# Cross-attention on one core: the token branch's last steps placed inside its loop and among the main branch's first tiles

## What is computed

```python
enc, ca = ctx[:, :2044], ctx[:, 2044:]            # ctx (2, 2048, 384), x (2, 1024, 640)
hs = mha(x @ Wq, enc @ Wk, enc @ Wv)              # 8 heads of 80
ca_q1 = einsum('btc,th->bch', ca, Wq_ca)[:, indices]   # 384 rows spread to 1024
ca_hs1 = mha(ca_q1, x, x)
ca_hs2 = mha(ca_hs1 @ Wq, ca @ Wk_ca, ca @ Wv_ca) # 4 keys
out = (hs + ca_hs2) @ Wout + b_out + x
```

## Time and profile before

| quantity | value |
|---|---|
| median of three runs | 1199.17 us |
| profiled execution, its own time | 1199.81 us |
| its span, first to last instruction | 1197.8 us |
| PE busy | 1189.5 us (99%) |
| DVE busy | 826.5 us (69%) |
| ACT busy | 680.4 us (57%) |
| POOL busy | 210.7 us (18%) |
| chain that ended last, PE's share | 95% |
| granted TensorE clock | 1.000 |

### The profile page before, as it was taken

The page is one execution under the profiler, slowest core; times in us unless marked ns, Lnnn a source line. Parts: engine busy times, 40 slices in busy tenths (PEclk is TensorE's granted clock), DMA queues, the critical chain, the costliest instruction groups (busy, mean ns, idle before and its releaser), DMA issues.

```text
span 1197.8 us, 14824 instructions
## 1 busy us (share of the span) xinstructions
PE 1189.5 (99%) x5649; PEld 965.1 (81%) x5649; DVE 826.5 (69%) x1181; ACT 680.4 (57%) x797; POOL 210.7 (18%) x123
## 2 busy tenths in 40 slices
PE   9999999999999999999999999999999999999999
PEld 7888888788666677888888888888888888888998
DVE  7468625771144388888888888888888888886551
ACT  5323433222644467777677777777777777778210
POOL 1100000011000021222222222222221221221233
PEclk9999999999999999999999999999999999999999
DMA  8975785693920084354454455445436436422254
GB/s 310 352 271 177 266 299 212 224 322 113 293 50 1 1 199 99 97 125 111 111 120 112 106 116 127 101 105 137 106 90 152 100 80 155 134 68 67 91 196 154
DMA packets 139376, 178.08 MB, mean 149 GB/s; under 512 B 79705, under 2 KB 97113, under 8 KB 135466
## 3 DMA queue, kind: packets, MB, share of 16 engines
q1 hardware_dynamic: 131690, 156.36, 46.1%
q0 software_dynamic: 2864, 10.24, 2.6%
q10 hardware_dynamic: 4752, 10.55, 2.6%
HBM read 113.72 MB, written 63.24 MB: 148 GB/s over the span
## 4 chain that ended last, share of the span: by engine, by line
PE 95%; DVE 2%; DMA 1%; issue 1%; ACT 1%; SPq 0%; DVEq 0%; ACTq 0%
PE at_ps L1330 28%; PE bank L726 20%; PE at_ps L1311 19%; PE at_ps L243 9%; PE acc_t_ps L1091 7%; PE at_ps L1520 6%; PE s_ps L1059 2%; PE bank L703 1%; DVE prob_lo L1186 1%; DMA x_f<-in_xT 1%; PE acc_t_ps L1070 1%; PE f_ps L243 1%; PE f_ps L1012 1%; PE f_ps L1022 0%; PE at_ps L1523 0%
## 5 line engine op out<-in xcount | busy, mean ns | idle before, releaser
L259 DVE TENSOR_REDUCE mpart<-at_ps 128x1 f32<-128x512 f32 x480 | 324.6, 685 | 90.8 <-PE at_ps L243 89.2
L1249 ACT ACTIVATE prob_hi<-at_ps 128x1024 fp32r<-128x1024 f32 (+1 forms) x256 | 263.3, 1028 | 178.9 <-PE at_ps L1311 176.8
L1330 PE MATMUL at_ps<-prob_hi,v 128*128 128x512 f32 (+1 forms) x1024 | 315.0, 393 | 0.0
L1186 DVE TENSOR_TENSOR prob_lo<-probs,prob_hi 128x1024 fp32r<-128x1024 f32 (+1 forms) x211 | 273.5, 1296 | 21.3 <-ACT probs L1254 20.7
L1254 ACT ACTIVATE probs<-at_ps 128x1024 f32<-128x1024 f32 (+1 forms) x256 | 261.6, 1022 | 0.0
L1330 PEld LDWEIGHTS at_ps<-prob_hi,v 128*128 128x128 f32 (+1 forms) x1024 | 191.1, 188 | 43.7 <-ACT x_hi_place L1263 1.7
L1186 POOL TENSOR_TENSOR prob_lo<-probs,prob_hi 128x1024 fp32r<-128x1024 f32 x45 | 108.0, 2400 | 501.6 <-ACT probs L1254 501.6
L243 PE MATMUL at_ps<-a 128*128 128x512 f32 x480 | 189.0, 394 | 0.4 <-DVE mpart L259 0.4
L1330 PE MATMUL at_ps<-prob_lo,v 128*128 128x512 f32 (+1 forms) x512 | 158.7, 391 | 0.5 <-DVE prob_lo L1186 0.5
L1311 PE MATMUL at_ps<-a 128*128 128x512 f32 (+1 forms) x512 | 158.7, 391 | 0.2 <-DVE vw L965 0.2
L1311 PE MATMUL at_ps<-b 128*128 128x512 f32 (+1 forms) x512 | 158.1, 390 | 0.0
(11 more groups left out here) (160 smaller groups left out, 1392.8 us busy)
## 6 DMA issues: line engine op xcount, KB each, us to landing
v_hi_d<-v_t SPq DMA_DIRECT2D x16, 648.0 KB, 6.3
v_lo_d<-v_t SPq DMA_DIRECT2D x16, 648.0 KB, 8.1
v<-v_hi_d SPq DMA_DIRECT2D x16, 648.0 KB, 5.5
v<-v_lo_d SPq DMA_DIRECT2D x16, 648.0 KB, 7.2
k_hi_d<-out_hi SPq DMA_DIRECT2D x40, 256.0 KB, 4.9
k_lo_d<-out_lo SPq DMA_DIRECT2D x40, 256.0 KB, 5.9
a<-k_hi_d SPq DMA_DIRECT2D x16, 640.0 KB, 7.6
b<-k_hi_d SPq DMA_DIRECT2D x16, 640.0 KB, 11.2
```

The costliest lines, as they stand in the source:

```text
L259: dve.tensor_reduce(self.mpart[:, g % 2, qt, c:c + 1], at[:, 0:w], AX, ALU.max).then_inc(self.mx_done, 1)
L1186: eng.tensor_tensor(pl[n % PL][0:r, :], prob[n % PF][0:r, :], ph[n % PB][0:r, :].bitcast(F32), ALU.subtract).then_inc(sem, 1)
L1249: act.activation(ph[n % PB][0:r, :], s_ps[n % 2][0:r, :], ACT.Exp, scale=SCALE).then_inc(ph_done, 1)
L1330: mm = pe.matmul(wide[3][:, u], a[0:r, t, :], y[0:r, u * CH:(u + 1) * CH], start=t == 0 and m == 0, stop=t == KT - 1 and m == 2)
```

## The change

- Maxima chunks start at token step 8 (`MAX_FROM` 2), and 16 chunks of head 1 (`AHEAD`) follow those of head 0, so that 49 steps carry one; the first two main steps carry none, the next ten one or two. Loads of the first two heads' `a` are issued earlier on SP. Chunks have 512 columns and last tiles 128 keys throughout; the four excess keys have zero values (`fill_ones` clears them, `load_v` leaves them out, with four DMAs a head for two).
- The gather of batch 1 stands in token step 57, in the maxima's PSUM banks (now one tensor, `f_both`); `fold_values` in steps 59 and 60. ACT's copies of them stand in the same steps.
- What is left of the token part (last token scores, last exponential, `weigh`, gather, copy) stands among main steps 0 and 1, as the functions of `TokensEnd`.
- `normalise` is two operations of 512 columns, at t = 10 and t = 11, each behind a wait for the low part of tile n + 1.
- `early_split` of t = 13 to 15 stands behind the last low part.

```diff
-MAX_FROM = 6
+MAX_FROM = 2
+GATHER_AT, VALUES_AT = 57, (59, 60)
+AHEAD = 16
-FIRST_PIECES = (2, 3, 2, 3, 3, 2, 3, 3, 2, 3, 3, 3)
+FIRST_PIECES = (0, 0, 1, 2, 1, 2, 1, 2, 1, 2, 2, 2)
...
-    def normalise(self, pool, g):
+    def normalise(self, pool, g, u):
         p = g % 2
+        half = slice(u * CH, (u + 1) * CH)
         pool.wait_ge(self.rbc_in, (g + 1) * 16)
-        pool.tensor_tensor(self.o_raw[p][0:D, :], self.o_raw[p][0:D, :], self.rbc[:], ALU.mult
+        pool.tensor_tensor(self.o_raw[p][0:D, half], self.o_raw[p][0:D, half], self.rbc[:, half], ALU.mult
                            ).then_inc(self.norm_done, 1)
...
@@ tokens, scalar
+                    if k == GATHER_AT:
+                        first_copy()
+                    if k in VALUES_AT:
+                        vw_out(VALUES_AT.index(k))
                 if n == NH:
-                    exp2(0)
+                    exp2(act, 0)
             raw_out(len(heads) - 1)
-            vw_out(0)
-            first_copy()
-            exp2(1)
-            vw_out(1)
...
@@ tokens, tensor, end of step k
+                if k == GATHER_AT:
+                    first_gather()
+                if k in VALUES_AT:
+                    fold_values(VALUES_AT.index(k))
-            pe.wait_ge(oh_done, 1)
-            pe.wait_ge(at.mx_done, STEPS)
-            fold_values(0)
-            token_scores(len(heads) - 1)
-            first_gather()
-            fold_values(1)
...
@@ attend, gpsimd
-                if t == 11 and g:
-                    at.normalise(pool, g - 1)
+                if t in (10, 11) and g:
+                    wait_low(pool, n + 1)
+                    at.normalise(pool, g - 1, t - 10)
...
@@ attend, scalar
             exp(0)
-            last_copy(act)
+            tokens_end.last_exp(act)
             exp(1)
+            tokens_end.last_copy(act)
...
@@ attend, vector
             split(0)
+            tokens_end.last_weigh(dve)
...
-                if g == G - 1:
+                if g == G - 1 and t < KT - 3:
                     early_split(dve, t)
+            for t in range(KT - 3, KT):
+                early_split(dve, t)
...
@@ attend, tensor
+            tokens_end.folded_values(pe)
+            scores(0, nothing)
+            tokens_end.last_scores(pe)
+            scores(1, nothing)
+            tokens_end.last_fold(pe)
+            values_high(0, nothing)
+            scores(2, nothing)
+            values_low(0)
+            values_high(1, nothing)
+            tokens_end.last_gather(pe)
+            scores(3, nothing)
+            values_low(1)
+            tokens_end.gathered(pe, B)
+            for n in range(2, N):
```

More of the change, by code:

```diff
@@ L779, in tokens @@
         raw = kept["raw"]
[L780 to L784, removed]
+        rden, s2, t2, r2 = kept["fold"]
+        f_both = s.psum("f_ps", [P, 2, CH])
+        f_ps = [f_both[:, i] for i in range(2)]
         s_ps = [s.psum(f"s_ps{i}", [P, 2, CH]) for i in range(2)]
@@ L997, in vector, with token_scores @@
                     if n == NH + 1:
-                        weigh(0, order[0])
-            low_vw(0)
+                        weigh(dve, 0)
+                if k in VALUES_AT:
+                    low_vw(VALUES_AT.index(k))
             fold(len(heads) - 1)
             center(order[1])
-            weigh(1, order[1])
-            low_vw(1)
+        def token_scores(pe, n):
+            b, h = heads[n]
+            if n == 0:
+                pe.wait_ge(wk2_done, B)
+            pe.wait_ge(raw_done, n + 1)
+            for c in range(KC):
+                mm = pe.matmul(t_ps[n % 2][:, c, :], raw[n % 2][:, c * P:(c + 1) * P],
+                               kept["wk2"][:, b, h, :], start=True, stop=True)
+            mm.then_inc(t_full, 1)
         def tensor(pe):
@@ L1114, in last_gather @@
             pe.wait_ge(p2_done, B)
-            pe.wait_ge(e_done, len(heads) * pairs)
             for c, a, z in spans:
@@ L1327, in values @@
                     for u in range(2):
-                        if t == 0 and m == 0 and g:
+                        if t == 0 and low == 0 and g:
                             pe.wait_ge(at.o_act, 2 * (g - 1) + u + 1)
-                        mm = pe.matmul(wide[3][:, u], a[0:r, t, :], y[0:r, u * CH:(u + 1) * CH],
-                                       start=t == 0 and m == 0, stop=t == KT - 1 and m == 2)
-                    if m < 2:
-                        between()
-                mm.then_inc(pv_done, 1)
@@ L1336, in tensor, with values_low @@
-            pe.wait_ge(at.kb_ones, 3)
-            gathered(pe, 1)
-            scores(0, lambda: None)
-            last_gather(pe)
-            folded_values(pe)
-            scores(1, lambda: None)
-            for n in range(N):
+                        pe.matmul(wide[3][:, u], v_s[g % 2][:, low, t, :], ph[n % PB][:, u * CH:(u + 1) * CH],
+                                  start=t == 0 and low == 0, stop=False)
+                    between()
+            def values_low(n):
+                g, t = divmod(n, KT)
+                wait_low(pe, n)
+                for u in range(2):
+                    mm = pe.matmul(wide[3][:, u], v_s[g % 2][:, 0, t, :], pl[n % PL][:, u * CH:(u + 1) * CH],
+                                   start=False, stop=t == KT - 1)
+                mm.then_inc(pv_done, 1)
@@ L1455, in gpsimd @@
                 add_bias(n)
-            at.normalise(pool, G - 1)
+            for u in range(2):
+                at.normalise(pool, G - 1, u)
             for n in range(2, NT_OUT):
@@ L1571, in program @@
         kept["p1_0"] = blocks(wq_flat[:, n_x:n_x + n_p], 2)
+        n_f = n_x + n_p
+        small = []
+        for shape in ((2, KC), (B, KC, HT), (B, KC * NH), (B, KC * NH)):
+            n = math.prod(shape)
+            flat = wq_flat[:, n_f:n_f + n]
+            names = "abc"[:len(shape)]
+            small.append(flat.rearrange(f"p ({' '.join(names)}) -> p {' '.join(names)}", **dict(zip(names, shape))))
+            n_f += n + -n % 8
+        assert n_f <= 2 * MC * HID
+        kept["fold"] = small
         kept["wkca"] = blocks(x_flat[:, 0:n_k], KC)
```

190 lines of the change are left out of this document (103 added, 87 removed).

## The result

The changed kernel takes **1225.95 us** (median of 4 runs, 1224.67 to 1227.83), the one before 1199.26 beside it: a ratio of 1.0224, 95% interval 1.0208 to 1.0240. The sign was forecast, the size was not: 1205.6 us, with a range that ended at 1207.5. The profiled execution took 1225.38 us. All times are medians of the runs that lie within 1.5% of their kernel's fastest, which leaves out one run, 1242.34 us of `e3_split_alone`.

A forecast was written before the change was run, and what follows sets the result against it. PE was taken to bound the kernel, so only removed matmuls or PE stops pay. Terms 0.1 + 4.5 + 2.55 - 3.4 + 2.8 - 0.5 + 0.4 gave +6.4 us: profiled 1206.2, median 1205.6, range 1199.3 to 1207.5.

The forecast's parts named there:

- Whole chunks and whole last tiles: 512-column chunks and 128-key last tiles in every head: -0.5 us in all, bounds -1.1 and +0.2; extra DMAs on SP free.
- Token steps 57, 59, 60: Token loop: ACT's copies delay exponentials, PE stops 1.6, 1.45 and 1.45 us; +4.5, bounds +1.3 and +5.4.
- The seam and the chunks: Between token and main attention: old stops go, -3.4, new ones +2.55; moving head 1's chunks of maxima into token steps, +0.1.
- The stop before scores 4: Seam: ACT's copy of the gather stands ahead of tile 2's exponentials, so PE waits 1.75 us.
- the wait for DVE's fold: Seam, behind the last token scores: DVE folds for 1.03 us and PE waits 0.4 us.
- that for the weights: Seam, behind high products 1: PE waits 0.4 us for DVE's weights, which take 1.76 us.
- Halves: Normalisation in 14 heads: POOL's second half holds up DVE's negation and the transpose; +0.2 a head, +2.8 us, bounds -2.8 and +4.2.
- The end: Last head: subtraction parts moved save 0.75, but the halves delay DVE's subtractions; +0.4 us net, bounds -0.75 and +1.5.
- Half blocked: Rival on the halves: negation not held, only tile 13's subtraction, a head costs as before; +3.6, 1202.8 us; chance 0.23.
- the cover holds: Rival on the halves: both lie beside reductions, -0.2 us a head; +0.8, 1200.0 us; chance 0.18.
- POOL's multiplication is the cause of all stops of a head: Faster rival: 0.42 us in 14 heads goes, head period under 43.8 us; -2.7, 1196.5 us; chance 0.11.
- the 0.42 us: PE's stops in each main head before the change: 44.18 us a head against 43.76 of bare work.

The follow-up runs named there:

- e3_split_alone: The kernel before with only the change's load_v (124 rows x 16 tiles and 4 rows x 15 tiles), matmuls unchanged: 1221.53 us, ratio 1.0181.
- v1: On e2, ACT's three copies in the token loop each made one exponential later, PE's order unchanged: 1199.57 us, ratio 1.0003.
- e2: The changed kernel with load_v's four DMAs a head cut as 128 rows x 15 tiles and 124 rows of the last tile: 1204.22 us, ratio 1.0043.
- v4_whole: On e2, the normalisation as one multiplication of 1024 columns at tile 11, as before the change: 1201.55 us, ratio 1.0020.
- e1_two_loads: The changed kernel with values loaded as before, two DMAs a head, and the last tile's values matmuls contracting 124 rows: 1204.92 us, ratio 1.0048.
- x124_only: The kernel before with load_v as one 124-row DMA each for high and low parts, the last four rows zeros: 1221.67 us, ratio 1.0184.

## Why the prediction was wrong

The step that failed is one sentence under *Whole chunks and whole last tiles*: "Two more DMAs a head are issued on SP where nobody waits for them; loading is far ahead of use." I counted the two new DMAs as the extra, and took the two large ones for what they were, since they lost 4 rows of 128. But these hold the cost, 10 us each in a later head. And SP's issues are in order: whoever waits for `mrow` waits for whatever stands ahead of it, however early that is loaded. With 28 us of loads the row of maxima was 11.5 us later on SP than before (470.02 against 458.49), and 7.3 later than with fast loads in the changed kernel (462.72); its transfer took 9.45 us on top. The error is 21.4 us of span, all of the miss and more: 15.9 by head 1's first tile (489.60 against 473.68), 4.9 in the 13 heads behind it, the rest behind those.

The rest, by spans (sum +6.4 forecast, +4.4 measured: 1202.2 against 1197.8):

- *Token steps 57, 59, 60*: +4.5 forecast, -4.65 when undone, and 1.63, 1.44 and 1.43 us by PE's starts at the three places, where 1.6, 1.45 and 1.45 were forecast. Mechanism and size right; the lower bound of 1.3, from the one form in the trace of before, was far off.
- *The seam and the chunks*: -3.4 + 2.55 + 0.1 = -0.75 forecast. The low products of head 1's first tile start 4.20 us later than before, of which 4.26 are the copies (in v1 it starts at 469.42 in place of 473.68), so about -0.1 is left. The stop before scores 4 was forecast as 1.75, and cost 1.66 in its row and 1.87 when undone; the wait for DVE's fold was forecast as 0.4 and is 0.20, that for the weights is not there. What the seam won was therefore nearer to 2 than to 3.4.
- *Halves*: right in mechanism (negation held, transpose late). That undoing them gave 2.7 us where 2.8 stood in the forecast is luck: 0.8 of it lies in the last head, which the forecast had apart, under *The end*. In the 14 heads it is 1.8 for 2.8: 13 heads take 574.73 us with halves and 572.95 with the whole, 0.14 a head where 0.2 was forecast (a head's period is 44.21, for 44.4), and what follows head 14's first tile takes 153.79 and 152.98.
- *Whole chunks and last tiles*: -0.5 forecast, bounds -1.1 and +0.2; measured -1.6, outside them. The bounds came from the last tile alone, and chunks of 508 columns lose as well, below.
- *The end*: +0.4 forecast. From head 14's first tile to the end it is 153.94 us before and 153.79 in e2: -0.15, in which the widths of two heads have their part. The last two steps of low products take 3.50 us before, 2.72 with one multiplication (`v4_whole`) and 3.53 with the halves (e2): the parts moved behind the last low part save 0.78, as forecast (0.75), and the two halves cost 0.81 there, where 1.15 were forecast.

That `e1_two_loads` lies only 0.7 us from the forecast's sum does not bear out each term: the seam gave 0.7 less than forecast, the widths 1.1 more, and the halves cost 1.0 less in their heads and 0.3 less at the end.

Of the rivals, none had this mechanism. "Half blocked" and "the cover holds" are refuted by the negation of 0.59 us. "POOL's multiplication is the cause of all stops of a head" was refused for the change as it is, rightly; but with the halves a tile earlier a head does fall to 43.8 us, the bound I had named for it, so POOL and the widths together did hold nearly all of the 0.42 us: 0.27 a head is the one multiplication (44.07 for 43.80 us) and 0.13 the widths.

## What to carry to other kernels

When a change touches the shape of a DMA, ask how many engines it will be dealt to, and price it by a row of that shape; here 124 rows were slow and 128, 120, 112, 64 and 60 were not. Read what stands *behind* it in the issuing queue, up to the next thing that somebody waits for; a byte count or a count of DMAs said nothing here. Sending the row of maxima ahead of the loads was not tried. An engine that works in order should not wait for late work ahead of work that others need: copies put one or two exponentials later gave back 4.65 and 1.87 us. And a short instruction at the head of a chain (a negation on eight columns) is worth keeping clear of POOL's, more than a long one that nobody waits for.

## What the runs showed of the hardware

- A DMA of 124 rows x 16 x 81 f32 moved some 65 GB/s at a DMA busy share of 0.31, and held the next on its queue for 9.5 to 10.7 us in the later heads (`x124_only`); with 128, 120, 112, 64 or 60 rows the longest row there is 5.64 us. In the loads of the first two heads, where much is queued, every kernel has a row of 8.4 us or more (14.43 and 11.35 before).
- Stops of PE of 5.2 (e3), 6.6 (`x124_only`), 8.8 (e3) and 13.5 us were each followed by some 4 us at clock 0.50. Of two near 3 us, the one of 2.96 (after, at 748.9) was followed by 1.00, the one of 2.82 (e3, at 473.1) by 0.68 over 3.2 us and 0.77 over the next 3. No stop in these kernels up to 1.7 us lowered it.
- Narrower matmuls are not cheaper here and break the pace: with chunks of 508 of 512 columns (8 of a head's 32) and a last tile of 124 rows, mean tile times are 2.728 against 2.720 us in the tiles with chunks alone, and 2.756 against 2.719 up to the last tile's low products; 13 heads take 571.28 us against 569.60. Which of the two widths has which share beyond these tile times wasn't tried.
